# Two attention and expert layers on one core: batch row 0's routing moved into the attention, and more experts computed sparsely

## The reference

```python
x = x + attn_a(layernorm(x))   # 16 heads of 8, latent keys and values, rotary part of 32, causal
x = x + ffn(layernorm(x))
x = x + attn_b(layernorm(x))   # 16 heads of 8, plain causal attention, no output projection
x = x + ffn(layernorm(x))

def ffn(x):                                        # 8 experts, hidden 512
    scores = softmax(x @ router_w.T)               # per token, over the experts
    capacity = int(1024 * 2.0 / 8) + 1             # 257
    gate_vals, sel_idx = top_k(scores_t, capacity) # per batch row and expert, over the tokens
    tokens = x[b_idx, sel_idx]
    y = gelu(tokens @ w1 + b1) @ w2 + b2           # exact gelu
    return zeros.at[b_idx, sel_idx].add(y * gate_vals)
```

## Time and profile before

| | us |
|---|---|
| median of 3 runs | 979.27 (978.05 to 980.05) |
| profiled execution | 978.48 |
| its span, first to last instruction | 976.6 |
| PE / DVE / ACT / POOL busy | 840.6 / 653.0 / 565.9 / 350.9 |
| attention a, up to | 336.5 |
| feed-forward 0 | 336.5 to 506.8 |
| attention b with its projection | 506.8 to 810.3 |
| feed-forward 1 | 810.3 to 976.6 |

### The profile page before, as it was taken

The page is one execution under the profiler, slowest core; times in us unless marked ns, Lnnn a source line. Parts: engine busy times, 40 slices in busy tenths (PEclk is TensorE's granted clock), DMA queues, the critical chain, the costliest instruction groups (busy, mean ns, idle before and its releaser), DMA issues. The chain is left out here.

```text
span 976.6 us, 15787 instructions
## 1 busy us (share of the span) xinstructions
PE 840.6 (86%) x5786; PEld 535.1 (55%) x5786; DVE 653.0 (67%) x1204; ACT 565.9 (58%) x1020; POOL 350.9 (36%) x579
## 2 busy tenths in 40 slices
PE   3888999999999889979937898999999988997992
PEld 1554566556655567769824333444444436676981
DVE  4686667767774457947745877777777745785772
ACT  2524666656666567746705256666666676775661
POOL 1262336656233300186826112133212330008683
PEclk9999999999999989989969799999999999997996
DMA  3662431331111151024424271110000006112444
GB/s 102 185 204 55 143 85 66 98 98 34 66 66 45 59 160 44 22 70 132 54 53 125 69 186 43 34 34 13 22 2 2 1 2 185 55 44 57 138 56 100
DMA packets 57595, 73.57 MB, mean 75 GB/s; under 512 B 11296, under 2 KB 44784, under 8 KB 57136
## 3 DMA queue, kind: packets, MB, share of 16 engines
q1 hardware_dynamic: 43024, 61.42, 21.5%
q0 software_dynamic: 7168, 5.45, 4.2%
q10 hardware_dynamic: 7328, 5.71, 2.1%
HBM read 41.68 MB, written 29.77 MB: 73 GB/s over the span
## 5 line engine op out<-in xcount | busy, mean ns | idle before, releaser
L1141 ACT ACTIVATE b_pt<-b_banks 128x512 f32<-128x512 f32 (+1 forms) x320 | 154.6, 559 | 100.1 <-PE b_banks L1055 99.9
L1164 DVE TENSOR_REDUCE a_mlate<-a_banks 128x2 f32<-128x1024 f32 (+3 forms) x120 | 125.0, 1080 | 50.8 <-PE a_banks L993 32.1
L1164 DVE TENSOR_REDUCE b_mlate<-b_banks 128x2 f32<-128x1024 f32 (+3 forms) x120 | 126.0, 1081 | 35.0 <-PE b_banks L993 18.3
L1055 PE MATMUL a_banks<-a_q,a_k 121*128 121x512 f32 (+3 forms) x384 | 117.4, 383 | 5.5 <-DMA a_q<-a_mt 4.6
L1141 ACT ACTIVATE a_q_hl<-a_banks 128x512 f32<-128x512 f32 (+1 forms) x160 | 81.8, 557 | 68.5 <-PE a_banks L1055 67.0
L1141 ACT ACTIVATE a_k_hl<-a_banks 128x512 f32<-128x512 f32 (+1 forms) x160 | 82.2, 557 | 52.8 <-PE a_banks L1055 51.3
L993 PE MATMUL a_banks<-a_k,a_q 120*128 120x512 f32 (+3 forms) x384 | 99.5, 362 | 11.0 <-DVE a_mlate L1164 7.3
L1055 PE MATMUL b_banks<-b_q,b_k 64*128 64x512 f32 (+3 forms) x384 | 98.1, 413 | 11.7 <-ACT b_pt L1141 8.9
L1659 ACT ACTIVATE f_h<-f_banks,b_t 128x512 f32<-128x512 f32 (+1 forms) x136 | 89.4, 685 | 30.3 <-PE f_banks L1594 17.0
L1055 PEld LDWEIGHTS b_banks<-b_q,b_k 64*128 64x128 f32 x384 | 47.1, 185 | 86.7 <-ACT b_pt L1141 55.3
L1055 PEld LDWEIGHTS a_banks<-a_q,a_k 121*128 121x128 f32 x384 | 65.3, 191 | 50.9 <-issue 20.1
(11 more groups left out here) (252 smaller groups left out, 1371.0 us busy)
## 6 DMA issues: line engine op xcount, KB each, us to landing
scratch_w<-a_tab SPq DMA_DIRECT2D x16, 512.0 KB, 3.0
f_w1r<-scratch_w SPq DMA_DIRECT2D x16, 512.0 KB, 4.5
f_w2r<-scratch_w SPq DMA_DIRECT2D x16, 512.0 KB, 3.6
a_rot<-in_w SPq DMA_DIRECT2D x16, 256.0 KB, 3.9
a_q<-scratch_q SPq DMA_DIRECT2D x8, 384.0 KB
a_k<-scratch_k SPq DMA_DIRECT2D x8, 384.0 KB
scratch_q<-b_q_hl SPq DMA_DIRECT2D x24, 128.0 KB, 2.8
b_q<-scratch_q SPq DMA_DIRECT2D x32, 96.0 KB
```

The source lines that it names most:

```text
L1055: last = pe.matmul(st[u % NST][:, col:col + w], head_rows(k2, n, h, slice(key * P, (key + 1) * P), 1), head_rows(q2, n, h, slice(c * CH + ...
L1141: act.activation(pt[at % NPT][:, h, 0:cols], st[u % NST][:, 0:cols], ACT.Exp, scale=scale).then_inc(exp_done, 1)
L1164: last = dve.tensor_reduce(dst, src, AX.X, ALU.max, negate=True)
```

## The change

- **Row by row.** Routing is done per batch row (class `Routing`): 8 columns in place of 16, with tensors that live through the whole kernel. The two rows' search steps, lists, gathers and scatters are separate.
- **Row 0 in the attention.** In both attentions row 0's join (in a also the projection), measure and scale stand at units 108 to 115 of the second batch row's 160 (`ROUTE_AT`, `ROUTE_VECTOR`), its norm on ACT at 117 to 120, turn at 123, logits at 127, softmax at 129 and 130, and 11 of the 15 search steps from 133 to 158, through the ring that the score pieces use. SP stores row 0's tokens and scores, and the zeros, there too.
- **Row 1 in the feed-forward.** Its projection, norm, logits, softmax and all 15 steps stand beside expert units, and so do the last 4 steps of row 0. PE begins with experts at once.
- **Experts.** Row 0 keeps experts 0 and 1 dense, row 1 expert 0: 6 dense items; the rest is sparse, 6 items for row 0 and 7 for row 1, of 258 columns. 19 items in all. `rows` of a sparse item stands 5 units ahead of its first unit (3 behind a dense item), `back` 17 units behind its first.
- **Lists.** For all experts of a row at once: two comparisons by digits of 128x1024, 16 matmuls (`find`) and 2 more (`expand`), in place of one 128x2048 comparison and 16 matmuls for each expert. By the new table `expand` stands at unit 18 for row 0 and 76 for row 1, the first `rows` at units 25 and 89; the last unit is 155.
- **Weights** have a buffer for each expert, loaded in order at the stage's start.
- **Sums**: two per batch row, for even and odd experts; each has its own chain of scatters. Row 0's are read back and added before the stage ends.

```diff
-KEEP = 3
-DENSE = KEEP * NCH
-ROUTED = NE - KEEP
...
-ITEMS = [("dense", q) for q in range(AHEAD)] + [("some", s) for s in range(ROUTED)]
-ITEMS += [("dense", q) for q in range(AHEAD, DENSE)]
+DIGITS = 16
+QUAD = 4
+LATE = range(NCH // B, NCH)
+KEEPS = (2, 1)
+ITEMS = [("dense", 0, 0), ("dense", 0, 1), ("dense", 1, 0), ("dense", 1, 1)] + [("some", 0, e) for e in range(KEEPS[0], NE)]
+ITEMS += [("dense", 0, 2), ("dense", 0, 3)] + [("some", 1, e) for e in range(KEEPS[1], NE)]
...
+KEPT_ROOM = 4
+TAKE_AT = {(4, 1): 2, (4, 3): 3}
...
+SOME_COST, DENSE_COST, STEP_COST, STEP_EVERY = 0.65, 0.95, 0.4, 2.1
+EARLY_STEPS = 11
+STEPS = len(SHIFTS)
...
+    for n, item in enumerate(ITEMS):
+        if item[0] == "some":
+            late = 0 if ITEMS[n - 1][0] == "some" else 2
+            at += [(unit_of(n - 1) + 3 + late, ("rows", *item[1:])), (unit_of(n + 2) + 1, ("back", *item[1:]))]
+    first = [(2 * i - 1, ("count", 0, EARLY_STEPS + i)) for i in range(STEPS - EARLY_STEPS)]
+    u = first[-1][0]
+    at += first + [(u + 2, ("rank", 0)), (u + 4, ("place", 0)), (u + 5, ("odd_index", 0)), (u + 11, ("find", 0)),
+                   (u + 13, ("expand", 0))]
+    at += [(13, ("xn", 2)), (14, ("xn", 3)), (18, ("logits", 1))]
+    steps = paced(22, [STEP_EVERY] * (STEPS + 1) + [1.0, 4.5, 1.2])
+    at += [(u, ("count", 1, i)) for i, u in enumerate(steps[:STEPS])]
+    at += list(zip(steps[STEPS:], [("rank", 1), ("place", 1), ("odd_index", 1), ("find", 1), ("expand", 1)]))
+    last = {b: max(ITEM["some", b, e] for e in range(KEEPS[b], NE)) for b in range(B)}
+    after = unit_of(last[0] + 2)
+    at += [(unit_of(6) + 3, ("twins", 0)), (after + 5, ("odd_turn", 0)), (after + 7, ("odd_sum", 0))]
+    for i, item in enumerate(KEPT):
+        b = item[2] // (NCH // B)
+        n = 5 + i if b == 0 else last[0] + 3 + i
...
+ROUTE_AT = {"a": [(108, ("attn_turn", 0)), (111, ("attn_out", 0))], "b": []}
+for _kind in "ab":
+    ROUTE_AT[_kind] += [(123, ("xn_turn", 0)), (127, ("logits", 0))]
+    ROUTE_AT[_kind] += [(133 + 5 * i // 2, ("count", i)) for i in range(EARLY_STEPS)]
+ROUTE_VECTOR = {"a": [(113, "measure", 0), (114, "measure", 1), (115, "scale", 0), (130, "weigh", 0)],
+                "b": [(110, "join", 0), (111, "measure", 0), (112, "join", 1), (113, "measure", 1), (115, "scale", 0),
+                      (130, "weigh", 0)]}
+ROUTE_SCALAR = [(117 + i, "norm", i) for i in range(TT // 2)] + [(129, "exp", 0)]
...
+    def logits(self, pe, to):
+        m = self.m
+        for i in range(TT):
+            last = pe.matmul(to[:, i * NE:(i + 1) * NE], m.xt[:, self.tile(i) * P:(self.tile(i) + 1) * P], m.rw_t[:, :],
+                             start=True, stop=True)
...
+    def count(self, pe, to, i):
+        m = self.m
+        pe.wait_ge(m.count_ready, self.counts + i + 1)
+        for t in range(TT):
+            last = pe.matmul(to[:, 0:(PLANES - 1) * NE], m.ones_b[:, :], m.reach[:, :, t, :], start=t == 0, stop=t == TT - 1)
+        return last
...
+    def expand(self, pe, to):
+        for c in range(B):
+            last = pe.matmul(to[:, c * P:(c + 1) * P], self.m.expand[:, c * P:(c + 1) * P], self.group, start=True, stop=True)
+        return last
...
+    def weigh(self, dve):
+        m = self.m
+        each = m.total[:, :].rearrange("p (t o) -> p t o", o=1).to_broadcast([P, TT, NE])
+        self.link(dve, dve.memset(m.limit[:, :], 0))
+        dve.wait_ge(m.exped, self.use + 1)
+        self.link(dve, dve.tensor_reduce(m.total[:, :], m.e_x[:, :, :], AX.X, ALU.add))
+        self.link(dve, dve.reciprocal(m.total[:, :], m.total[:, :]))
+        dve.tensor_tensor(self.score[:, :, :], m.e_x[:, :, :], each, ALU.mult).then_inc(m.scored, 1)
+        self.reach_out(dve, 0)
...
+    def lists(self, dve):
+        m = self.m
+        dve.tensor_scalar(m.high_digit[:, :, :], m.slot[:, :, :], 4, None, ALU.logical_shift_right)
+        self.link(dve, dve.tensor_scalar(m.low_digit[:, :, :], m.slot[:, :, :], DIGITS - 1, None, ALU.bitwise_and))
+        numbers = m.steps[:, len(SHIFTS) * PLANES:].rearrange("p (o n) -> p o n", o=1).to_broadcast([P, TT * NE, DIGITS])
+        digit = lambda t: t.rearrange("p t (e o) -> p (t e) o", o=1).to_broadcast([P, TT * NE, DIGITS])
+        self.link(dve, dve.tensor_tensor(self.pairs[:, :, 1, :], numbers, digit(m.high_digit[:, :, :]), ALU.is_equal))
+        dve.tensor_tensor(self.ends, numbers, digit(m.low_digit[:, :, :]), ALU.is_equal)
+        self.link(dve, dve.tensor_scalar(self.pairs[:, :, 0, :], self.pairs[:, :, 1, :], m.token[:, 0:1], None, ALU.mult))
+        ones = self.pairs.rearrange("p (t e) v a -> p t e v a", e=NE)[:, :, :, 1, :]
+        rows = m.tile_row[:, :].rearrange("p (t o q) -> p t o q", o=1, q=1)
+        dve.tensor_tensor(ones, ones, rows.to_broadcast([P, TT, NE, DIGITS]), ALU.mult).then_inc(m.hot_ready, 1)
...
+        early.store_rows(sp, norm)
+        early.store_scores(sp)
...
+        def route_entry(key):
+            what, i = key
+            if what == "attn_turn":
+                pe.wait_ge(ring_done, RING["o", LAST[NG - 1]] + 1)
+            elif what in ("attn_out", "logits"):
+                pe.wait_ge(ring_done, RING["route", "attn_turn" if what == "attn_out" else "xn_turn", 0] + 1)
+            to = slot(("route", *key))
...
+        def norm_tiles(first, end):
+            act.wait_ge(norm.scaled, NCH // B)
+            for t in range(first, end):
+                act.activation(m.xn[:, t, :], m.x[:, t, :], ACT.Identity, scale=m.sc[:, 2, t:t + 1], bias=m.sc[:, 3, t:t + 1]
+                               ).then_inc(norm.xn_by_act, 1)
...
+            if what in ("attn_turn", "xn_turn"):
+                dve.tensor_copy(m.xt[:, 0:TT * P], mx[at % 2][:, :, :].rearrange("p b w -> p (b w)")).then_inc(ring_done, 1)
+            elif what == "attn_out":
+                x = m.x[:, 0:TT, :].rearrange("p t n -> p (t n)")
+                dve.tensor_tensor(x, x, mx[at % 2][:, :, :].rearrange("p b w -> p (b w)"), ALU.add).then_inc(ring_done, 1)
+                dve.wait_ge(ring_done, at + 1)
+            elif what == "logits":
+                early.compare(dve, source, ring_done)
+            else:
+                early.step(dve, source, done, i)
...
+        for e in range(4):
+            weights(e)
+        late.store_rows(sp, norm)
+        for e in range(4, NE):
+            weights(e)
+        late.store_scores(sp)
+        sp.wait_ge(m.listed, late.use + 1)
+        reload(sp, 0, 0)
...
+        early.wait_lists(pool)
+        early.gather_odd(pool)
+        for e in experts[0]:
+            gather(0, e)
+        pool.wait_ge(m.filled, 16 * 4 * (k + 1))
+        for e in experts[0][:-2]:
+            scatter(0, e)
+        late.wait_lists(pool)
+        late.gather_odd(pool)
+        gather(1, experts[1][0])
+        gather(1, experts[1][1])
+        scatter(0, NE - 2)
+        gather(1, experts[1][2])
+        scatter(0, NE - 1)
+        for e in experts[1][3:]:
+            gather(1, e)
+        scatter_odd(0)
+        for e in experts[1]:
+            scatter(1, e)
+        scatter_odd(1)
...
+        beside(-1)
+        for u in range(LAST_UNIT):
+            n, j = divmod(u + HB, 2 * HB) if u >= HB else (0, u)
+            if j < HB and n < len(ITEMS):
+                hidden(n, j)
+            elif j >= HB:
+                output(n - 1, j - HB)
+            beside(u)
+        for u in range(LAST_UNIT, LAST_UNIT + 2 * HB):
...
+        def finish(b):
+            for c in range(b * NCH // B, (b + 1) * NCH // B):
+                dve.wait_ge(m.x_in[c], 32 * (k + 1))
+                early.link(dve, dve.tensor_tensor(flat(m.x, c), flat(m.x, c), landing(c, 0).rearrange("p t n -> p (t n)"), ALU.add))
+                dve.tensor_tensor(flat(m.x, c), flat(m.x, c), landing(c, 1).rearrange("p t n -> p (t n)"), ALU.add
+                                  ).then_inc(finished, 1)
```

1317 lines of the change are left out of this document (632 added, 685 removed).

## The result

| | before | after |
|---|---|---|
| median, first series (4 runs each) | 978.66 (977.29 to 980.05) | 996.88 (988.69 to 1001.34) |
| ratio, 95% interval | | 1.0187, 1.0118 to 1.0256 |
| profiled execution | 978.48 | 988.69 |
| attention a | 336.5 | 351.0 |
| feed-forward 0 | 170.3 | 161.3 |

All in us. The kernel became slower, as forecast. The profiled execution lies 3.6 above the forecast of 985.1 for it, but the median lies 8 higher still: it rose by 18.2 us where 6 were forecast. The runs of the changed kernel also lie far apart. Two things have to be explained: the stages, and the spread.

What follows compares the result with a forecast made beforehand. GpSimd's gathers and scatters behind the row lists bound the feed-forward, VectorE the time until row 1's lists. From the profiled 978.5 us: +6.5 − 5.8 + 9.5 − 2.6 − 1 = +6.6, so 985.1; range 980 to 1001.

Steps and rivals of the forecast that it cites:

- GpSimd's chain: Feed-forward, behind row 1's lists: 15 gathers and 20 scatters issued in about 60.5 us, setting the stage's end.
- VectorE's block: Attention, around row 0's projection: copies, measures and scale need 6.6 to 7.5 us where 1.5 to 2 are free; 3.5 stalls.
- Row 1's lists at 90 and 93 us: Feed-forward: VectorE limits when row 1's lists are ready, 90 us into the second stage, 93 into the first.
- The gather exposed as it is now, 4.56, 3.04 and 1.83 us: Feed-forward: row 0's first gathers stay as slow as before, leaving TensorE idle about 5 us.
- The tail 1 us shorter in all: End of the feed-forward stages: four additions still follow the reload, half the output leaves early, 1 us less.
- First expert matmul 5 us in: Feed-forward start: with the head gone only the first weight load remains, taken as 5 us.
- Table loads 2.6 us: Feed-forward, row 1's softmax between Gelus: two more table loads per stage, 2.6 us of ScalarE, 1.5 us of delay.
- The attention, +6.5 and +9.5: Row 0's work inserted in the last third lengthens the first attention by 6.5 us and the second by 9.5.
- (a): Rival, feed-forward: VectorE keeps up, row 1's lists come before 87 us, each stage gains 10 us more; 958 us, chance 0.19.
- (b): Rival: the attention absorbs the insertions, +3 and +3 instead of 16, stages as forecast; 975 us, chance 0.14.
- (c): Rival, feed-forward: the saved matmul time shows in full, 26 + 10.8 us less per stage; 921 us, chance 0.02.
- (d): Rival, feed-forward: scatters slow beside a busier VectorE, 0.6 us more for each of 35 issues; 1025 us, chance 0.06.

Runs made afterwards that it cites:

- no_turns: Changed kernel without the additions of batch row 0's four dense results on VectorE (one-column copies instead): 988.56 us, ratio 1.0100 against the kernel before.
- pace: Changed kernel with row 1's search steps closer together and its gathers ahead of row 0's last four experts' scatters: 1002.12 us, ratio 1.0277 against the kernel before.
- beside_scatters: Changed kernel plus 12 unread VectorE operations per stage beside GpSimd's late issues, subtractions in the first feed-forward, copies in the second: 997.97 us, ratio 1.0239.
- five_scatters: Changed kernel without batch row 1's scatters for experts 6 and 7 in each stage: 977.86 us, ratio 0.9998 against the kernel before.
- again: The changed kernel, unedited, run and profiled a second time: 995.95 us median of six runs, ratio 1.0215 against the kernel before.
- no_measure: Changed kernel without VectorE's measure and scale of batch row 0 in both attentions: 988.15 us, ratio 1.0092 against the kernel before.
- bare: Changed kernel without row 0's measure and scale, ScalarE norms (one column stays) and 11 search steps in both attentions: 974.37 us, ratio 0.9972 against the kernel before.
- after: The changed kernel, unedited, in its first profiled execution: 988.69 us; median of that first series 996.88 us, ratio 1.0187 against the kernel before.
- wake: Kernel before, with GpSimd setting one column of a small tile after six search steps to stay awake: 976.84 us, ratio 0.9988 against the kernel before.

## Why the prediction was right, and where it was wrong

Of the forecast of 985.1 for the profiled execution the feed-forward stages hold −9.4 and the attentions +16; measured −16.2 and +26.5. The errors, −6.8 and +10.5, largely cancel, so that the 3.6 us are luck; by the medians the kernel lost three times what was forecast. Direction and the two mechanisms, GpSimd's chain and VectorE's block in the attention, are as forecast; the sizes of the attention's terms are not.

- **Row 1's lists at 90 and 93 us.** 88.5 and 93.0, and the first gather 1.65 us later, at 90.1 and 94.7, behind expert 5's scatters. `no_turns` shows that VectorE's work counts in front of them (4.6 and 2.8 us for 4.5), and `pace` that closer steps bring the lists 6 us earlier and the stage's end later. But VectorE was busy 0.76, not over 0.8: its queue decides through TensorE's waits for comparisons and slots (11.4 us in two rows), more than through its own fullness.
- **The gather exposed as it is now, 4.56, 3.04 and 1.83 us.** Wrong. I took them for the price of a first gather; what lengthened them were the operations of VectorE beside them, the comparisons of `make_hot` first, which the change replaces. (The ends of the gathers and the added subtractions of `beside_scatters` say so; no run takes the comparisons out of the kernel before.) Nothing waited for gathered rows; a wait of 4.9 us for row 0's slots took the place of the 5 us, so the sum held by luck.
- **GpSimd's chain of 60.5 us without a pause.** 58.5 and 58.0, some 0.06 us less for each issue. (The prediction starts it at 91.5 in the text and at 91.0 in its sum, half a microsecond apart.) `five_scatters` shows that it ends the stages.
- **The tail 1 us shorter in all.** From the last issue to the next stage 8.1 us for 9.9, and 11.0 for 12.2 at the end: 3 us less.
- **First expert matmul 5 us in.** 4.0 (355.01), with 2.2 us of wait for the weights.
- **Table loads 2.6 us.** One of the two has nothing behind it, and the other stands as before right ahead of a Gelu, with no drain:

```profile
389.68 0.69 ACT L1857 ACTIVATE f_ykeep<-f_banks,b_t 128x512 f32<-128x512 f32 x1
390.39 1.28 ACT L1834 ACT_TABLE_LOAD   x1
391.68 1.27 ACT L1834 ACTIVATE f_h<-f_banks,b_t 128x512 f32<-128x512 f32 x2
```

- **The attention, +6.5 and +9.5.** This is the step that failed in size. The terms by the table (`again`): the stall behind VectorE's block, said 3.5, is 5.0 in each; `no_measure` gives 3.1 and 4.5 of it, and in `bare`, without the norms too, 0.0 and 0.7 are left. One reading behind it was off: VectorE was busy for 12.47 of 18 us, 0.69 and not 0.66. The projection was to cost nothing since its matmuls only move. It costs 3.3 in attention a: it came from the tail, where TensorE has waits to hide it in, to units 104 to 112, where it has none, and between units 136 and 144, where it stood before, 1.6 to 2.5 came back. No run leaves it out by itself. Norms, turn, logits and steps were to cost 3 and 6; from unit 120 on it is 3.5 and 7.9. That is 11.8 and 13.0 in `again`, whose granted clock from unit 112 on was 0.94 to 0.97 in attention a, but 0.72 to unit 120 and 0.90 behind it in attention b, where the kernel before had 0.99 to 1.00: part of b's terms is clock.
- **The clock.** Absent from the forecast. The granted clock falls in the last third behind TensorE's waits (the attentions' mean from 0.98 and 0.96 to 0.96 and 0.93), and the executions part there: 3.8 us between `after` and `again` in attention a, 6.5 to 9.0 in b where the long stretch occurs. This is the likely reason why the median lies 8 us above the profiled execution, whose clock is the highest of its four (0.926, against 0.906, 0.920 and 0.925). What starts the long stretch in one execution and not in another stays open.
- **The rivals.** (a), lists before 87 us, did not occur (88.5 and 93.0). (b) is excluded by the table, (c) by `five_scatters`. (d) as priced, 0.6 us more for each issue, did not occur, but I dismissed its mechanism wrongly: the rows that I had called cold were the evidence for it.'s mean hid them, and hid two gathers of 1.94 and 2.22 us in the very stretch from 425 to 447.5 that I named against it.

## What to carry to other kernels

Work moved from a stage's start into a stretch beside other work costs there what its slowest queue lacks in room: price each engine's block against the ring that its neighbours share, and count what a full engine gives up for a tail in which it had waits to spare. Where GpSimd issues transfers, lay VectorE's timeline beside the slow issues before calling them cold. Look at several executions' clocks before you trust one profile: here one execution of the changed kernel is 8 us under its median.

## What the runs showed of the hardware

- GpSimd's issue of a gather or scatter was lengthened by two-operand SBUF operations of VectorE beside it: 4.56, 3.04 and 1.83 us against 0.94 in `before` and `wake`, 2.52 against 1.56 in `beside_scatters`. Not each such overlap does it (0.94 at 444.04).
- The executions of one kernel can part into groups: six of the changed kernel at 988 to 991 (granted clock 0.926 to 0.929) and 1001 to 1005 (0.906). Four edited kernels' longer executions have a stretch of some 38 us at 1.2 GHz in the last third of attention b; the traces of the changed kernel's shortest executions have none.
